# A Mamba scan laid out as 8 images x 16 channels instead of 16 x 8, with its saves on ScalarE

## What is computed

```python
def _mamba(u, ...):                      # u: 16 images, 3136 pixels, 48 channels
    xm, z = jnp.split(einsum('bld,ed->ble', u, in_w), 2, axis=-1)
    xm = silu(conv1d(xm, c1_w, padding=2 before) + c1_b)
    dt_r, Bm, Cm = split(einsum('bld,ed->ble', xm, xp_w), [3, 19], axis=-1)   # 3, 16, 16
    dt = softplus(einsum('blr,dr->bld', dt_r, dt_w) + dt_b)
    A = -exp(A_log)                      # 48 channels x 16 states
    def step(h, (dt_t, x_t, B_t, C_t)):  # over the 3136 pixels
        h = exp(dt_t[..., None] * A) * h + (dt_t * x_t)[..., None] * B_t[:, None, :]
        return h, einsum('bdn,bn->bd', h, C_t)
    y = (scan(step) + xm * Dp) * silu(z)
    return einsum('bld,ed->ble', y, out_w)
```

## Time and profile before

| what | value |
|---|---|
| time, median of 3 runs | 4541.69 us (4536.73 to 4549.5) |
| the profiled execution's own time | 4543.22 us |
| its span, first to last instruction | 4541.4 us |
| Mamba block, first tap load to last result copy | 1113 to 2743 us |
| first to last scan | 1286.9 to 2688.0 us |
| DVE busy, whole span | 2889.2 us (64%) |
| ACT busy | 2697.7 us (59%) |
| PE busy | 3671.0 us (81%) |
| POOL busy | 1604.2 us (35%) |
| loads of B and C | 28 + 28 of 896 KB |
| saves on DVE (L1425) | 168 |

### The profile page before, as it was taken

How to read it: one execution, slowest core, us unless ns; L and a number is a source line. 1 busy time by engine, 2 the same in 40 slices (tenths; PEclk the granted TensorE clock), 3 DMA queues, 4 the chain that set the end, 5 groups by cost and what they waited for, 6 DMA issues and landing times. The chain is left out here.

```text
span 4541.4 us, 73738 instructions
## 1 busy us (share of the span) xinstructions
PE 3671.0 (81%) x20680; PEld 2129.8 (47%) x20680; DVE 2889.2 (64%) x4573; ACT 2697.7 (59%) x4664; POOL 1604.2 (35%) x1446
## 2 busy tenths in 40 slices
PE   3599999986668788888887667789999877699956
PEld 1288888733223333333333223344444333699932
DVE  1266666665059998898989965646666666111146
ACT  2355555576656676776766326767777667233336
POOL 0033333300246676676767640025555500000000
PEclk7699999988879999999999988999999989799979
DMA  2100000022453655646463312200000012200012
GB/s 65 34 14 15 14 15 14 14 53 68 113 154 94 167 146 146 169 122 166 122 171 102 101 55 55 53 15 15 16 15 15 9 45 60 51 13 11 11 42 53
DMA packets 202998, 296.56 MB, mean 65 GB/s; under 512 B 68542, under 2 KB 188526, under 8 KB 202098
## 3 DMA queue, kind: packets, MB, share of 16 engines
q1 hardware_dynamic: 193654, 285.57, 23.9%
q10 hardware_dynamic: 9216, 9.65, 0.9%
HBM read 193.01 MB, written 102.03 MB: 65 GB/s over the span
## 5 line engine op out<-in xcount | busy, mean ns | idle before, releaser
L1472 POOL TENSOR_TENSOR mam_hc<-mam_h,mam_cs 128x896 f32<-128x896 f32 x336 | 711.9, 2124 | 337.3 <-DVE mam_h L1415 323.8
L1203 PE MATMUL mam_ps_y<-mam_hc,mam_ident 128*128 128x448 f32 x1344 | 634.7, 600 | 207.7 <-POOL mam_hc L1472 207.7
L1415 DVE TENSOR_TENSOR_SCAN mam_h<-mam_a,mam_kept,mam_dbx 128x448 f32<-128x448 f32 x672 | 729.4, 1124 | 2.2 <-ACT mam_a L1319 2.1
L1319 ACT ACTIVATE mam_a<-mam_ft,mam_a_neg 128x448 f32<-128x448 f32 x672 | 402.2, 656 | 244.0 <-DVE mam_h L1415 243.3
L1846 POOL TENSOR_TENSOR scan_ch<-scan_h,scan_cs 128x392 f32<-128x392 f32 x256 | 350.1, 1384 | 554.5 <-DVE scan_h L1812 554.5
L1203 PEld LDWEIGHTS mam_ps_y<-mam_hc,mam_ident 128*128 128x128 f32 x1344 | 262.5, 206 | 548.1 <-POOL mam_hc L1472 329.2
L1402 DVE TENSOR_TENSOR mam_dbx<-mam_ps_u,mam_bs 128x448 f32<-128x448 f32 x672 | 381.9, 611 | 83.8 <-DMA mam_cs<-dram_bc 82.3
L658 POOL TENSOR_TENSOR att_prob<-att_prob,att_share 128x588 f32<-128x588 f32 x128 | 151.7, 1185 | 451.9 <-DVE att_share L843 451.9
L440 PE MATMUL f_xc_ff<-all_x,f_centre 128*128 (+1 forms) x288 | 150.5, 608 | 177.4 <-DVE all_x L319 147.9
L1812 DVE TENSOR_TENSOR_SCAN scan_h<-scan_turned_in,scan_start 128x392 f32<-128x392 f32 x192 | 251.7, 1328 | 29.5 <-ACT scan_turned_in L1731 27.0
L1686 PE MATMUL scan_ps_merged<-scan_ch,scan_w_merge 128*128 128x392 f32 x512 | 230.7, 532 | 46.0 <-POOL scan_ch L1846 43.5
(11 more groups left out here) (207 smaller groups left out, 7995.2 us busy)
## 6 DMA issues: line engine op xcount, KB each, us to landing
mam_taps<-normed SPq DMA_DIRECT2D x1008, 43.5 KB
mam_bs<-dram_bc SPq DMA_DIRECT2D x28, 896.0 KB, 11.4
mam_cs<-dram_bc SPq DMA_DIRECT2D x28, 896.0 KB, 16.9
normed<-f_staged SPq DMA_DIRECT2D x512, 38.1 KB
mam_ft<-dram_steps SPq DMA_DIRECT2D x42, 448.0 KB, 4.9
f_mixed<-mixed SPq DMA_DIRECT2D x384, 36.8 KB
dram_gs<-mam_gs SPq DMA_DIRECT2D x56, 224.0 KB, 2.8
mam_gt<-dram_gs SPq DMA_DIRECT2D x56, 224.0 KB
```

Of the source, the lines that this page charges most:

```text
L1203: mm = pe.matmul(ps_y[p % 2][:, 0:MT], ident[:], hc[t % 2][:, i, :], start=False, stop=(t % 8 == 7 and i == 1))
L1319: act.activation(a[t % 3][:, i, :], ft[p % 2][:, 0, :], ACT.Exp, scale=a_neg[:, at:at + 1]).then_inc(decays, 1)
L1415: dve.tensor_tensor_scan(h[:, n % 8, :], a[t % 3][:, i, :], dbx[:, i, 0:MT], kept[:, at:at + 1], ALU.mult, ALU.add).then_inc(scanned, 1)
L1472: pool.tensor_tensor(hc[t % 2][:], h[:, row:row + 2, :], cs[:, 2 * pair:2 * pair + 2, :], ALU.mult).then_inc(weighed, 1)
```

## The change

Lanes become 8 images x 16 channels (DL = 16). A stage falls into two sides of 8 images each (SIDES = 2), and what was a stage for the scan is now a span, a side of a stage: 3 passes, 24 steps, four rounds, four items ("duos"). There are 14 spans; passes (42) and steps (336) stay. The front must be one span ahead, so LEAD falls to 7 and LAG to 6, and there are 70 rounds. B and C are loaded for each span, from 8 images instead of 16, each row to 16 lanes instead of 8. `kept` holds 2 x 48 columns as before (96). The saves move from DVE to ACT, into ACT's slot two steps before the scan that needs them; the scan now waits for the save of the four rows it is about to overwrite. `carry` moves on POOL from k=1 of the inner item's round to k=4 of the round before, when ACT has just gated the item.

```diff
-DB = D // 8
-PASSES = STAGES * DB
+DL = 16
+DB = D // DL
+SIDES = 2
+SI = IMAGES // SIDES
+SPANS = STAGES * SIDES
+PASSES = SPANS * DB
 STEPS = PASSES * 8
...
-LEAD = 11
-LAG = 10
+LEAD = 7
+LAG = 6
...
-                def load_bc(s, g):
+                def load_bc(span, g):
+                    s, side = divmod(span, SIDES)
                     if g == 0:
-                        sp.wait_ge(bc_out, 16 * DUOS * (s + 1))
-                    reached(sp, weighed, 8 * DB * (s - 1) + 8 * (DB - 1) + 2 * g + 2)
+                        sp.wait_ge(bc_out, 16 * DUOS // SIDES * (span + 1))
+                    reached(sp, weighed, 8 * DB * (span - 1) + 8 * (DB - 1) + 2 * g + 2)
                     for tile, row in ((bs, 4 * g), (cs, STATES + 4 * g)):
                         sp.dma_start(tile[:, 4 * g:4 * g + 4, :],
-                                     bc_d[:, s, row:row + 4, :].rearrange("i r n -> i (r n)"
-                                     ).unsqueeze(1).to_broadcast([IMAGES, 8, 4 * MT])
+                                     bc_d[SI * side:SI * side + SI, s, row:row + 4, :].rearrange(
+                                         "i r n -> i (r n)").unsqueeze(1).to_broadcast(
+                                             [SI, DL, 4 * MT])
                                      ).then_inc(bc_in[g], 16)
...
-                        if (t + 5) % 48 in (0, 2, 4, 6) and 0 <= (t + 5) // 48 < STAGES:
-                            load_bc((t + 5) // 48, (t + 5) % 48 // 2)
+                        if (t + 5) % 24 in (0, 2, 4, 6) and 0 <= (t + 5) // 24 < SPANS:
+                            load_bc((t + 5) // 24, (t + 5) % 24 // 2)
...
+                def save(t):
+
+                    p, pair = divmod(t, 8)
+                    at = p % (SIDES * DB) * STATES + 2 * pair - 2
+                    row = (2 * t - 2) % 8
+                    act.wait_ge(scanned, 2 * t + 2)
+                    act.activation(kept[:, at:at + 4], h[:, row:row + 4, MT - 1], ACT.Copy
+                                   ).then_inc(saved, 1)
+
...
                         t = 6 * j + k + 2
                         if 0 <= t < STEPS:
                             decay(t)
+                        if t % 2 == 0 and 0 <= t - 3 < STEPS:
+                            save(t - 3)
...
                         if t % 2 == 0:
-                            reached(dve, saved, (t - 48) // 2 + 1)
+                            reached(dve, saved, t // 2 - 1)
...
-                        if t % 2 == 0 and 0 < t <= STEPS:
-                            save(t - 1)
...
-                        if k == 1 and inner is not None:
-                            carry(inner)
+                        if k == 4 and front is not None:
+                            carry(front)
                         if k == 4 and inner is not None:
                             clip(inner)
```

More of the change, by code:

```diff
@@ L894, in mamba_phase @@
         buf = Buffers(nc, ctx, "mam")
-        steps_d = nc.dram_tensor("dram_steps", [STAGES, DB, P, 2, MT], F32, kind="Internal").ap()
-        zs_d = nc.dram_tensor("dram_zs", [STAGES, DB, P, MT], F32, kind="Internal").ap()
-        ys_d = nc.dram_tensor("dram_ys", [STAGES, DB, P, MT], F32, kind="Internal").ap()
+        steps_d = nc.dram_tensor("dram_steps", [SPANS, DB, P, 2, MT], F32, kind="Internal").ap()
+        zs_d = nc.dram_tensor("dram_zs", [SPANS, DB, P, MT], F32, kind="Internal").ap()
+        ys_d = nc.dram_tensor("dram_ys", [SPANS, DB, P, MT], F32, kind="Internal").ap()
         gs_d = nc.dram_tensor("dram_gs", [ITEMS, P, MT], F32, kind="Internal").ap()
@@ L1019, in keep_rows @@
                 def keep_rows(dram, tile, m, sem):
-                    s, q = divmod(m, DUOS)
+                    span, q = divmod(m, DUOS // SIDES)
                     for i in range(2):
-                        lanes = 8 * (2 * q + i)
-                        sp.dma_start(dram(s)[:, lanes:lanes + 8, :],
+                        lanes = DL * (2 * q + i)
+                        sp.dma_start(dram(span)[:, lanes:lanes + DL, :],
                                      tile[HALF * i:HALF * i + D, :]).then_inc(sem, 16)
@@ L1079, in load_gated @@
                 def load_gated(r):
-                    s, q = divmod(r, DUOS)
+                    span, q = divmod(r, DUOS // SIDES)
                     if q == 0:
                         for p in range(2):
-                            sp.wait_ge(y_out[p], 16 * (DB // 2) * (s + 1))
-                        sp.wait_ge(gs_out, 16 * DUOS * (s + 1))
+                            sp.wait_ge(y_out[p], 16 * ((DB * (span + 1) + 1 - p) // 2))
+                        sp.wait_ge(gs_out, 16 * DUOS // SIDES * (span + 1))
                     reached(sp, mixed_out, r - 1)
@@ L1087, in load_gated @@
                     for i in range(2):
-                        lanes = 8 * (2 * q + 1 - i)
+                        lanes = DL * (2 * q + 1 - i)
                         sp.dma_start(yt[r % 2][HALF * i:HALF * i + D, :],
-                                     ys_d[s, :, lanes:lanes + 8, :]).then_inc(yg_in[r % 2], 16)
+                                     ys_d[span, :, lanes:lanes + DL, :]).then_inc(yg_in[r % 2], 16)
                     sp.dma_start(gt[r % 2][:], gs_d[r]).then_inc(yg_in[r % 2], 16)
@@ L1407, in scan @@
                     n = 2 * t + i
-                    at = p % DB * STATES + 2 * pair + i
+                    at = p % (SIDES * DB) * STATES + 2 * pair + i
                     dve.wait_ge(driven, n + 1)
@@ L1417, in scan @@
                                            ).then_inc(scanned, 1)
[L1419 to L1426, removed]
                 def times_z(p):
@@ L1501, in _ @@
                 for j in range(FIRST, LAST):
-                    inner, previous = item(j + LEAD - 1), item(j + LEAD - 2)
+                    front, inner = item(j + LEAD), item(j + LEAD - 1)
+                    previous = item(j + LEAD - 2)
                     for k in range(6):
@@ L2084, in mamba_layout @@
     w["mb_wx_dt"], w["mb_wdt"] = xp[0:DT_RANK], a["L1_conv_m_dt_proj_w"].T
-    a_log = a["L1_conv_m_A_log"].reshape(DB, 8, STATES).transpose(1, 0, 2).reshape(8, DB * STATES)
-    w["mb_a_log"] = np.tile(a_log, (IMAGES, 1))
-    w["mb_skip"] = np.tile(a["L1_conv_m_D"].reshape(DB, 8).T, (IMAGES, 1))
+    a_log = a["L1_conv_m_A_log"].reshape(DB, DL, STATES).transpose(1, 0, 2)
+    w["mb_a_log"] = np.tile(a_log.reshape(DL, DB * STATES), (SI, 1))
+    w["mb_skip"] = np.tile(a["L1_conv_m_D"].reshape(DB, DL).T, (SI, 1))
 def four_scan_layout(a, w):
```

8 lines of the change are left out of this document (4 added, 4 removed).

## The result

| | before | after |
|---|---|---|
| time, median of 4 runs each | 4543.2 us (4536.7 to 4549.5) | 4760.9 us (4760.1 to 4770.3) |
| ratio, 95% interval | | 1.0484 (1.0464 to 1.0504) |
| span of the profiled execution | 4541.4 us | 4768.5 us |
| start of the first scan, end of the last | 1286.9, 2688.0 us | 1233.1, 2933.3 us |

The change makes the kernel 4.8% slower; 4498 had been forecast, and 4548 was the upper end of the range. Scanning starts 54 us earlier and then takes 299 us longer; the tail is 18 us shorter. The loss lies between the first and the last scan.

What follows compares the result with a forecast made beforehand. Scan rounds with projections were taken as bound by a ring through POOL, PE, ACT, POOL and DVE, those without by DVE. Terms -61 -7 +9 -19 +4 -5 -3 +59 -20 = -43 gave a 4498 us median; range 4452 to 4548.

Steps and rivals of the forecast that it cites:

- The reloads: B/C loads inside the scan: 13 instead of six, same bytes a group, DMA engines full; +59 us.
- The prediction's own sign of being wrong: Windows with a reload differing from those of the kernel before (108 us) by more than 4 us.
- dear reload: Scan: ten reloads, j=8 to 44, at 10.9 us each; those at j=48 and 52 nearly free, +2 together.
- Rival B: Scan reloads cost more, ten bursts behind SP's queue with the taps; at 17 us each 4559; chance 0.15.
- Four head rounds less and the carry: Head: LEAD 11 to 7, -61 us; PE's wait for POOL's tails copy goes in about three rounds, -7.
- floor of 12.85: Head: SP idles only 2.45 of a 15.3 us round, so no round can be shorter than 12.85.
- Saves: Copies from DVE to ACT: 0 gained in rounds with projections; ACT's part costs +0.2 us for 46 rounds, +9.
- the ring from S to S: Scan rounds with projections: chain through POOL, PE, ACT, POOL, DVE between scan ends of steps 6j+2; 23.2 us, saves not in it.
- Rival A: Scan rounds: the ring doesn't bind, DVE's order does, so all saves' time returns; 4419; chance 0.10.
- Rounds without projections: Last six scan rounds (j = 50 to 55), DVE-bound: 3 saves go each, 1.03 us a save; -19.
- Tail: After the last scan: LAG falls from 10 to 6, four rounds of 5.0 us less; -20.

Runs made afterwards that it cites:

- lanes_swapped: Kernel after with lanes ordered channel * 8 + image instead of image * 16 + channel, so row transfers and B/C loads use 16 DMA engines: 4453.5 us.
- rows on 3: lanes_swapped with padded DRAM buffers, so stores of step, z, xm rows and loads of y run on 3 DMA engines; B/C loads stay on 16: 4619.0 us.
- stores3: lanes_swapped with eight unused DRAM rows behind each channel block, so stores of step, z and xm rows run on 3 engines, y loads on 16: 4561.2 us.
- lanes_swapped_g3: lanes_swapped with the last of a reload's four B/C load groups issued one slot earlier, ahead of the taps loads: 4407.3 us.
- lanes_swapped_bc8: lanes_swapped with each B/C load split into two DMAs of 64 lanes, on 8 engines, rows staying on 16 (table row "loads on 8"): 4595.1 us.

## Why the prediction was wrong

**The step that failed** is in *The reloads*: "a reload writes 128 x 4 x 448 words a group as before; only its source has 8 images instead of 16". The bytes were right. That the source's 8 images change nothing in the time was taken for granted, and the stores, whose slowest dimension fell from 6 to 3, weren't looked at. Everything after it (24 MB in 95 us at 250 GB/s, bursts that don't collide) assumes full engines. The prediction's own sign of being wrong, a window with a reload more than 4 us off, is there: 126 us against 108. Excess of 24 steps with a dear reload over four rounds of 23.4, means of 7 to 9 of them by ends of scan steps:

| | 24 steps | excess |
|---|---|---|
| forecast | | 10.9 |
| lanes_swapped | 102.4 | 8.8 |
| loads on 8 | 111.8 | 18.2 |
| rows on 3 | 114.4 | 20.8 |
| after | 125.2 | 31.6 |

So the term was sound for 16 engines and 20.7 us short for those of the kernel after, ten times 207 us. Of the 263 us between 4498 and 4761 some 14 more are in the head and 2 in the tail; the rest, about 40, is in the other rounds of the scan, by the ends of its rounds mostly in the milder reloads (the one at j=52 runs in rounds that DVE could have done in 19). Rival B had the right place and sign, and its "every microsecond on a dear reload is 10 us" held; its price of 17 didn't. Its reasons don't make the difference: as many bursts with as much traffic behind the same taps cost 8.8 us each in lanes_swapped. The queue does hold SP up in the kernel after, but in lanes_swapped, where the transfers are spread, it doesn't.

The Trainium skill states the rule that spoke against this change ("DMA: Bandwidth & Descriptors", section "Why a DMA increments its semaphore by 16 and not by 1"): a transfer runs on the largest number of engines up to 16 that divides the slowest dimension of both sides, on the lowest-numbered ones, and the unused ones' increments are made at once. The update counts agree in each kernel: 16, 9, 7, 4 and 3 for 16, 8, 6, 3 and 2. I had not set it against the shapes of the diff.

**Four head rounds less and the carry** (-61, -7). The first scan comes 54 us earlier, not 68; in lanes_swapped it comes at 1214.8, 72 earlier. By their taps, four rounds in the middle of the head are 13.6 to 15.0 us apart (12.2 to 15.5 before) and 10.6 to 12.4 in lanes_swapped; the one behind them takes 20.4 and 15.7. My floor of 12.85 by SP's issues holds for stores at 0.7 us each; on 16 engines they take 0.4 (medians 0.69 and 0.42). PE doesn't wait for the tails any more, as forecast. What is late next is a store: ACT, and PE behind it, wait for `gs` to land. From the waits of the kernel after between 1113 and 1233:

```profile
ACT mam_xg L1261 <- DMA dram_gs<-mam_gs: 18.9, 5, 6.7
```

The carry alone, on the kernel before, gave 12: there five of eleven head rounds fell from 15.2 to 15.5 us to 13.1 to 13.6. What its term gave in the new head of seven rounds, no run shows.

**Saves.** Right. DVE and ACT of the kernel after in rounds without a reload:

```profile
2310.57 1.48 DVE L1447 SCALAR_TENSOR_TENSOR mam_dt<-mam_ln,mam_consts,mam_es 128x448 f32<-128x448 f32 x1 [2.46 <-issue]
...
2333.98 1.49 DVE L1447 SCALAR_TENSOR_TENSOR mam_dt<-mam_ln,mam_consts,mam_es 128x448 f32<-128x448 f32 x1 [1.89 <-issue]
```
```profile
2324.28 0.19 ACT L1334 ACTIVATE mam_kept<-mam_h 128x4 f32<-128x4 f32 x1
...
2331.64 0.19 ACT L1334 ACTIVATE mam_kept<-mam_h 128x4 f32<-128x4 f32 x1
```

The copies' time turned into a wait of 1.9 to 2.5 us before `step_size`; the ring from S to S stays. The view names no releaser, but the second `step_size` (2333.98) starts 0.1 us after POOL has ended `series`:

```profile
2332.76 1.13 POOL L1500 TENSOR_TENSOR mam_es<-mam_es,mam_rv 128x448 f32<-128x448 f32 x1
```

Rival A is refuted: the saves alone gave 31 us, not some 100. On DVE a save took from 0.15 to 2.0 us, median 0.99; the mutual exclusion of DVE and POOL that rival A speaks of may be why, but no run isolates it. Freeing that time gains only where DVE is the bound. On ACT a save takes 0.19 us.

**Rounds without projections** (-19). DVE's slots are 3.1 us as forecast. The last 24 steps take 81.5 us in lanes_swapped, 2.4 of them a wait for a load, against 91.5 before. In the kernel after the last reload falls into these rounds and takes 16 us of it back:

```profile
L1419 DVE TENSOR_TENSOR mam_dbx<-mam_ps_u,mam_bs 128x448 f32<-128x448 f32 x46 | 26.2, 615 | 16.2 <-DMA mam_cs<-dram_bc 16.1
```

**Tail** (-20). Right: from the end of the last scan to that of the last result copy 37 us against 55.

**The whole** without the failed step: lanes_swapped, which is the change with every transfer spread, took 4454, within 1% of 4498 and just inside the range. The time without the failed step was thus 44 us too high: dear reloads at 8.8 instead of 10.9 are 21 of it, the head 4, the tail 3, and about 16 lie in other rounds of the scan, unassigned. That it spreads the rows over 16 engines, where the kernel before used 6, may have a part in that.

## What to carry to other kernels

When a layout changes, write down the slowest dimension of both sides of every DMA that it touches, stores and small ones too: a change that moves the same bytes can halve the engines. A dimension that has to be small belongs inside; a stride-0 broadcast or rows merged at one stride can stand outside as 16 or 48. A quick sign in a profile is a DMA share well under 1 while an engine waits for DMAs, and issues that hold their queue for several microseconds.

## What was not expected of the hardware

A confined transfer slows one that isn't. `dram_gs`, a store of 224 KB that is issued right behind the stores of xm and z rows, runs on 16 engines in every kernel. Its median time to landing, from the pages of after and of lanes_swapped (here with `mam_ft`, a load on 16 engines too):

```profile
mam_ft<-dram_steps SPq DMA_DIRECT2D x42, 448.0 KB, 7.2
...
dram_gs<-mam_gs SPq DMA_DIRECT2D x56, 224.0 KB, 8.0
```
```profile
mam_ft<-dram_steps SPq DMA_DIRECT2D x42, 448.0 KB, 3.8
...
dram_gs<-mam_gs SPq DMA_DIRECT2D x56, 224.0 KB, 3.4
```

For `dram_gs` the stores on 3 engines alone do it: it takes 7.8 us in stores3, and 3.3 and 3.2 with only y on 3 or only B and C on 8. `mam_ft` is weaker evidence, since it has 6.1 in lanes_swapped_g3 with every transfer spread: what is issued ahead of it counts as well. By the rule of the Trainium skill above, a transfer over 16 shares the lowest-numbered engines with the confined ones, and would end with its part behind them; no view here names an engine, so this reason is not shown.

The loads on 8 engines still moved 249 GB/s at a share of 0.69 between 1771 and 1781 in lanes_swapped_bc8, while others ran on 16. So a rate near the peak doesn't show that a transfer is spread; the count of updates does.

The two confinements added: 311 us together, 307 as a sum. An overlap had been the other possibility on record, as both fall into the same reloads.
